# Late attention of a four-block fused kernel: the next rows' transpose moved from slot 7 to slot 0, queries and keys moved to the outputs' bank, the first rows one chunk sooner

## What is computed

```python
x = x + jnp.tanh(g_xattn[2]) * _L2_xattn_ref(_layernorm(x), ctx_512, ctx_512, Wc, bc)
x = x + jnp.tanh(g_ffn[2])   * _L2_ffn_ref(_layernorm(x), ...)            # top-2 of 8 low-rank experts
x = x + jnp.tanh(g_xattn[3]) * _L3_xattn_ref(_layernorm(x), ctx_512, Wq, Wkv_expand, Wout)
x = x + jnp.tanh(g_ffn[3])   * _L3_ffn_ref(_layernorm(x), ...)            # top-2 of 8 adapters

# L2: queries are the normalised rows, keys and values the context, 16 heads of 16
scores = jnp.einsum('bghsd,bgtd->bghst', qh, kh) * scale
# L3: qp = q @ Wq.T; k, v = split(latent_kv @ Wkv_expand.T); scores are causal
attn = jax.nn.softmax(jnp.where(causal, scores, min), axis=-1)
out = jnp.einsum('bhqk,bhkd->bhqd', attn, vh).reshape(b, sq, H) @ Wout.T
```

## Time and profile before

| | us |
|---|---|
| median of 3 runs | 814.8 (810.33 to 816.83) |
| the profiled execution, device time | 817.1 |
| its span, first to last instruction | 815.3 |
| PE busy in the span | 754.6 (93%) |
| late stage, first slot to the end of the span | 572.1 to 815.3 |
| mean granted PE clock | 0.971 of full speed |

### The profile page before, as it was taken

The page is one execution under the profiler, slowest core; times in us unless marked ns, Lnnn a source line. Parts: engine busy times, 40 slices in busy tenths (PEclk is TensorE's granted clock), DMA queues, the critical chain, the costliest instruction groups (busy, mean ns, idle before and its releaser), DMA issues.

```text
span 815.3 us, 13192 instructions
## 1 busy us (share of the span) xinstructions
PE 754.6 (93%) x4753; PEld 595.5 (73%) x4754; DVE 505.6 (62%) x1171; ACT 356.2 (44%) x1178; POOL 191.3 (23%) x230
## 2 busy tenths in 40 slices
PE   6899999999999999999997889998889898898986
PEld 3688888888888888767775656886556676676764
DVE  5757455976875735455558653432877675665853
ACT  2121112111111111567675565222988686677851
POOL 0000031000000000000005990234354644535110
PEclk9989999999999999999999899999999999999998
DMA  8856100000003000400000004002222175275200
GB/s 245 302 162 211 25 0 1 1 1 0 1 1 107 1 0 1 146 1 1 2 1 2 1 10 63 1 1 72 72 72 66 42 109 94 69 117 98 66 15 26
DMA packets 53409, 44.95 MB, mean 55 GB/s; under 512 B 6641, under 2 KB 48609, under 8 KB 53217
## 3 DMA queue, kind: packets, MB, share of 16 engines
q1 hardware_dynamic: 53344, 44.11, 20.9%
HBM read 37.94 MB, written 6.16 MB: 54 GB/s over the span
## 4 chain that ended last, share of the span: by engine, by line
PE 74%; ACT 11%; DVE 8%; issue 4%; POOL 1%; DMA 1%; SPq 1%; ACTq 0%; POOLq 0%; DVEq 0%
PE PS L1679 22%; PE PS L1705 11%; ACT arena L1001 4%; PE PS L1768 3%; PE PS L1844 3%; ACT arena L931 3%; PE PS L1933 3%; PE PS L1784 2%; PE PS L1800 2%; PE PS L1812 2%; PE PS L1859 2%; PE PS L1827 2%; ACT arena L811 2%; PE PS L1959 2%; PE PS L2022 2%
## 5 line engine op out<-in xcount | busy, mean ns | idle before, releaser
L625 POOL TENSOR_TENSOR RS<-MV,eps 128x2 f32<-128x2 f32 x32 | 6.3, 197 | 546.3 <-DVE MV L1114 448.6
L811 ACT ACTIVATE arena<-PS 128x256 f32<-128x256 f32 (+3 forms) x192 | 102.7, 565 | 66.8 <-PE PS L1768 37.6
L1001 ACT ACTIVATE arena<-PS,W_d 128x256 f32<-128x256 f32 (+1 forms) x256 | 111.4, 460 | 13.3 <-DVE W_d L1395 11.2
L871 ACT ACTIVATE tanh_g<-PS 128x512 f32<-128x512 f32 x48 | 28.7, 597 | 170.1 <-PE PS L1679 170.1
L1679 PE MATMUL PS<-XT,W_g 128*128 128x256 f32 (+1 forms) x400 | 97.6, 387 | 0.0
L1679 PE MATMUL PS<-XT,W_u 128*128 128x256 f32 (+1 forms) x400 | 95.0, 379 | 0.0
L1705 PE MATMUL PS<-W_d,mlp_tmp 128*128 128x256 f32 (+1 forms) x400 | 93.9, 380 | 0.0
L1679 PEld LDWEIGHTS PS<-XT,W_u 128*128 128x128 f32 (+1 forms) x400 | 75.6, 190 | 11.2
L1705 PEld LDWEIGHTS PS<-W_d,mlp_tmp 128*128 128x128 f32 (+1 forms) x400 | 75.6, 190 | 10.3
L1679 PEld LDWEIGHTS PS<-XT,W_g 128*128 128x128 f32 (+1 forms) x400 | 75.2, 192 | 10.6 <-issue 0.8
L931 ACT ACTIVATE arena<-PS,arena 128x256 f32<-128x256 f32 x128 | 58.9, 477 | 15.4 <-DVE arena L1341 13.3
(11 more groups left out here) (226 smaller groups left out, 1362.3 us busy)
## 6 DMA issues: line engine op xcount, KB each, us to landing
NW<-scratch SPq DMA_DIRECT2D x64, 64.0 KB, 2.4
PM<-scratch SPq DMA_DIRECT2D x64, 64.0 KB, 2.4
W_d<-in_w_d SPq DMA_DIRECT2D x1, 3072.0 KB, 10.6
scratch<-W_d SPq DMA_DIRECT2D x16, 192.0 KB, 3.8
arena<-in_wq SPq DMA_DIRECT2D x4, 512.0 KB, 7.3
arena<-in_wo1T SPq DMA_DIRECT2D x4, 512.0 KB, 9.2
W_g<-in_w_g SPq DMA_DIRECT2D x2, 1024.0 KB, 12.5
W_u<-in_w_u SPq DMA_DIRECT2D x2, 1024.0 KB, 14.5
```

The source lines that it names most:

```text
L811: last = act.activation(dst, src, ACT.Copy)
L1001: last = act.activation(PL[:, n % 2, k * S:k * S + w], PS[:, bank + x, i * S:i * S + w], ACT.Exp, bias=NML[:, n % 2, k:k + 1], accum_out=D ...
```

## The change

- The transpose of the next rows is no longer issued two rounds ahead in slot 7 (and once in slot 0 of round 0), but for every round r+1 in slot 0 of round r, behind that slot's transposes and values. ACT copies it out behind the exponentials of slot 0.
- The query projection of the next causal round moves from slot 0 to slot 1, behind its transposes, and from bank 7 to bank 6. ACT copies it out at the head of slot 2.
- The keys move from slot 6 to slot 5, to bank 6, and are copied out at the head of slot 6, no longer ahead of its exponentials.
- POOL splits every round's queries at the head of its round r loop; SP issues queries r+1, then keys r+2. Two waits are added for the keys: SP's for `key_stacked` of the keys before and for the last scores of round r-2, POOL's for `key_stored`.
- The rows of round 0 are transposed behind chunk 16 and not 17, and split into `KP` in place of `XB[0]`, which the ternary stage still reads.

```diff
@@ late_fills (the same moves stand in ACT's and PE's loops)
-        if n == 0:
-            order.append((7, "turn", 1, 0))
-        if p == 0 and ahead and causal(r + 1):
-            order.append((7, "q", r + 1, 0))
...
+        if p == 0 and ahead:
+            order.append((7, "turn", r + 1, 0))
+        if p == 1 and ahead and causal(r + 1):
+            order.append((6, "q", r + 1, 0))
...
-        if p == 6 and r + 2 < ROUNDS and causal(r + 2):
-            order.append((7, "k", r + 2, 0))
+        if p == 5 and r + 2 < ROUNDS and causal(r + 2):
+            order.append((6, "k", r + 2, 0))
...
-        if p == 7 and r + 2 < ROUNDS:
-            order.append((7, "turn", r + 2, 0))
...
-TERNARY_TURN = [b * CH1 + 2 for b in range(NB - 1)] + [(NB - 1) * CH1 - 1]
+TERNARY_TURN = [b * CH1 + 2 for b in range(NB - 1)] + [(NB - 1) * CH1 - 2]
@@ SP
             def stack_keys(r):
                 sp.wait_ge(key_parts, r - NB + 1)
+                if r > NB:
+                    sp.wait_ge(key_stacked, 16 * len(PRODUCTS) * (r - NB))
...
+                bank, value = fill_at("late", "s", r - 2, PAIRS - 1)
+                sp.wait_ge(filled[bank], value)
...
             stack_queries(0)
-            stack_queries(1)
             for r in range(ROUNDS - 1):
-                if causal(r + 1):
-                    stack_queries(r + 1)
-                if r + 2 < ROUNDS:
-                    if causal(r + 2):
-                        stack_keys(r + 2)
-                    else:
-                        stack_queries(r + 2)
+                stack_queries(r + 1)
+                if r + 2 < ROUNDS and causal(r + 2):
+                    stack_keys(r + 2)
@@ ACT
-                if n == 0:
-                    late_queries(1)
-                if p == 0 and ahead and causal(r + 1):
+                if p == 2 and ahead and causal(r + 1):
                     late_queries(r + 1)
+                if p == 6 and r + 2 < ROUNDS and causal(r + 2):
+                    evacuate("late", "k", r + 2, 0,
+                             (KC[r % 2], PS[:, 6, :].rearrange("p (c s) -> p c s", c=2)))
...
                 if n + 2 < ITEMS:
                     late_exponents(n + 2)
+                if p == 0 and ahead:
+                    if causal(r + 1):
+                        xt_out(fill_at("late", "turn", r + 1)[1], (r + 1) % 2)
+                    else:
+                        late_queries(r + 1)
@@ PE
+                if p == 0 and ahead:
+                    late_turn(r + 1)
+                if p == 1 and ahead and causal(r + 1):
+                    late_query(r + 1)
...
-                if p == 6 and r + 2 < ROUNDS and causal(r + 2):
+                if p == 5 and r + 2 < ROUNDS and causal(r + 2):
                     late_keys(r + 2)
                 if p == 7:
                     denominators_turn(r)
-                if p == 7 and r + 2 < ROUNDS:
-                    late_turn(r + 2)
```

More of the change, by code:

```diff
@@ L577, in stack_queries @@
                     sp.dma_start(q_store[r % 2][:, c * P:(c + 1) * P, :].rearrange("k p t -> p k t"),
-                                 XB[r % 2][:, :, c * S:(c + 1) * S]).then_inc(query_stored[c], 16)
+                                 (XB[r % 2] if r else KP)[:, :, c * S:(c + 1) * S]).then_inc(query_stored[c], 16)
                 for c in range(2):
@@ L730, in query_parts_of @@
                 for c in range(2):
-                    x, (high, mid, low) = XT[r % 2][:, c, :], [XB[r % 2][:, k, c * S:(c + 1) * S] for k in range(3)]
+                    x, (high, mid, low) = XT[r % 2][:, c, :], [(XB[r % 2] if r else KP)[:, k, c * S:(c + 1) * S] for k in range(3)]
                     at = 3 * (2 * r + c)
@@ L745, in key_parts_of @@
                 pool.wait_ge(drained[bank], value)
+                if r > NB:
+                    pool.wait_ge(key_stored, 16 * (r - NB))
                 at = 3 * (r - NB)
@@ L762, in _ @@
             add_bias(1, bc_2)
-            query_parts_of(1)
             for r in range(ROUNDS + 1):
-                if r + 1 < ROUNDS and causal(r + 1):
+                if r + 1 < ROUNDS:
                     query_parts_of(r + 1)
@@ L779, in _ @@
                         add_bias(r + 2, bc_2)
-                        query_parts_of(r + 2)
         @block.scalar
@@ L1061, in _ @@
                     evacuate("late", "o", (n - 1) // PAIRS, c, (OTR[:, c, :], PS[:, 6, 0:S]))
-                if p == 6 and r + 2 < ROUNDS and causal(r + 2):
-                    evacuate("late", "k", r + 2, 0,
-                             (KC[r % 2], PS[:, 7, :].rearrange("p (c s) -> p c s", c=2)))
                 if p == 7:
                     evacuate("late", "den_turn", r, 0, (RDT, PS[0:NH, 7, 0:S]))
-                if p == 7 and r + 2 < ROUNDS:
-                    if causal(r + 2):
-                        xt_out(fill_at("late", "turn", r + 2)[1], r % 2)
-                    else:
-                        late_queries(r + 2)
                 if n + 2 < ITEMS:
                     late_exponents(n + 2)
+                if p == 0 and ahead:
[3 more added lines that the diff above has]
+                        late_queries(r + 1)
                 if p == 4 and ahead and causal(r + 1):
@@ L2097, in _ @@
                     late_scores(n + 2)
-                if n == 0:
-                    late_turn(1)
-                if p == 0 and ahead and causal(r + 1):
-                    late_query(r + 1)
                 if p == 1 and r:
```

## The result

The changed kernel takes 827.9 us (median of 4 runs, 825.8 to 830.4) beside 815.8 of the kernel before (810.3 to 817.9, 4 runs): ratio 1.016, 95% interval 1.010 to 1.022. It is slower by more than 1%, where I had forecast 818 with 824 as the upper end. The profiled execution took 827.6 us with a span of 825.8, 10.5 more than the span before; its mean granted clock is 0.968, before 0.971. PE is busy 756.1 us in place of 754.6, so nearly all of the difference is time in which PE stands still (both traces have stretches of slow clock, which largely cancel in this sum). A trace tells of one execution: of 19 runs of the kernel before, the fastest took 810.5 us at a mean granted clock of 0.985, the slowest 818.2 at 0.971.

A forecast was written before the change was run, and what follows sets the result against it. PE was taken to set the pace, through standstills and slow clock. Terms -1.2 (causal) + 2.1 (rounds 1 and 2) + 3.3 (round 1's queries) - 1.2 (first rows) + 0.5 (round 6) = +3.5 us on 814.8: 818, range 807 to 824.

The forecast's parts named there:

- The bank 6 moves cost nothing either: Queries and keys in bank 6: each earlier content is copied out before the next user comes, so no cost.
- the stall in slot 1: PE waits ahead of the denominators for ACT's copy of the rows: 1.9 us, six times, in rounds 1 to 6.
- Rounds 1 and 2: Denominators begin 1.05 us later in each: 2.1 us lost, up to 1 more each if the clock falls.
- I take it that the clock falls again: Causal rounds: slow clock, 1.5 us each, returns behind slot 1's stalls, leaving a gain of 0.3 each, 1.2 in all.
- the first rival: The clock does not fall behind the new stalls in slot 1: about 811 us, chance 0.22.
- The first rows: Round 0's rows, turned one chunk sooner in the ternary stage, shorten the later wait for stacks: 1.2 us gained.
- The keys' added waits: The two waits added on SP and POOL are fulfilled when reached: no cost.
- The queries of round 1: Slot (0,6): stacks come later, PE's wait grows from 1.33 to 3.6 us; with slow clock 3.3 us lost.
- round 6, where I had allowed 0.5: Round 6, with no keys in slot 5 and shorter slots: 0.5 us of wait for stacked queries, from 0 to 1.5.
- the chain: From POOL's start on the queries to the stacks that PE waits for: 12.3 us.
- could give at most: Upper limit in the steady part: slot 7's turns cost 9.8 us of waits plus 6 of slow clock, about 16.
- The third rival: Stacked queries come too late in rounds 3 to 5, 3.1 us of wait each: 827 us, chance 0.13.

The follow-up runs named there:

- e2: The changed kernel, but ACT copies the projected queries in slot 1, ahead of the expert weights' copy and that slot's exponentials: 819.9 us, ratio 1.006.
- d1: The changed kernel, but DVE does the choice of experts in slot 0 behind that slot's maxima, not in slot 7 ahead of them: 821.8 us, ratio 1.006.
- w1: The changed kernel, but POOL waits for the maxima of the next slot 0 before it splits the keys: 828.4 us, ratio 1.019.
- f10: The changed kernel with ten unused matmuls into bank 6 where PE waits in slot 1 for the rows' copy, six times: 819.0 us, ratio 1.004.
- e4: The kernel before, with only the rows of round 0 turned one chunk sooner and split into KP: 814.1 us, ratio 0.997.
- e3: The changed kernel, but round 1's rows are turned and copied at the head of slot 0 of round 0, as before: 824.8 us, ratio 1.010.
- k6: The kernel before, with only the keys moved to slot 5 and bank 6, the turn left in slot 7: 806.4 us, ratio 0.988.
- e123: The changed kernel with turned rows copied ahead of slot 0's exponentials, queries copied in slot 1, round 1's rows turned as before: 798.6 us, ratio 0.979.
- e1: The changed kernel, but in slot 0 ACT copies the turned rows ahead of that slot's exponentials: 802.8 us, ratio 0.983.
- e12: The changed kernel with turned rows copied ahead of slot 0's exponentials and projected queries copied in slot 1: 799.2 us, ratio 0.980.

## Why the prediction was wrong

Against the span, 10.5 us came where 3.5 were forecast. The direction and the main exchange (a stall in slot 7 for one in slot 1) were right, two steps were not, and the rest is size.

**The step that failed** is "The bank 6 moves cost nothing either: the outputs of slot 0 are copied before the queries come, the queries before slot 4". The next user of bank 6 behind the queries is not slot 4's output. The values of slot 2 fill it already, and between the projection and its copy ACT had the job's product and a set of exponentials. That makes four waits, 6.0 us, which the prediction had put at nothing. All four are gone in e2, which moves that one copy and is 8 us faster. I had looked at who ends in the bank, not at who begins in it.

**The term mis-sized** is the stall in slot 1. The stall itself is there six times in the place forecast, and 1.88 and 1.87 us of rounds 1 and 5 are what slot (7,0) gave. The other four are 2.23, 2.88, 2.47 and 2.77. That is 14.1 in place of 11.4. The profile that I read had no turn and no key splitting in slot (7,0), so I took ACT's list to be the only bound. In rounds 2, 3, 4 and 6 ACT waited 0.2 to 1.0 us for DVE's maxima, behind the job's choice; in three of these DVE itself was held by POOL's splitting of the keys. d1 takes all of it away, w1 the part due to POOL.

**Rounds 1 and 2.** Price 1.05 us each, and "with one up to 1 more each", one being a fall of the clock. Round 1 came out at it (4.48 with the queries, forecast 4.35). The stretch from (1,3) to (2,3) cost 3.85: 1.05, 0.3 for the longer stall, 1.0 for the clock at 0.53 behind it, as allowed, and 1.6 for the fall in slot (1,6), behind a wait that the change did not make. That last part is chance as far as the traces show.

**The clock.** "I take it that the clock falls again": it fell at four of the six stalls in slot 1 (rounds 2, 3, 5 and 6), and stayed at 1.00 behind those of 1.88 us in round 1 and 2.47 in round 4. So (3,3) to (4,3) is the one causal round that became shorter, by 1.0 us. f10 prices the falls at 9 us. The choice was right for three of the four causal rounds that I took it for, and the first rival (no fall, 811) is refuted.

**What was right.** The first rows: -1.25 for -1.2, and no slow clock behind their stacks (e4; the agreement to 0.05 us is luck, as such traces differ by 2 us at this slot). The keys' added waits cost nothing that a trace shows. The queries of round 1: PE's wait for PM 3.33 us for 3.6 (e3). No wait at L1627 for a copy in slot 7, one of 1.78 us for DVE's rows at the last ternary turn. No wait for stacks in rounds 3 to 5, and none in round 6, where I had allowed 0.5. But not by the sum that I gave: ACT copied the queries late, so POOL started 12.5 to 17.0 us into the rounds and not at 11.7. The scores came 11.0 to 13.8 us behind POOL's start and found the stacks there, in round 6 in less than the 12.3 us of the chain that I had reckoned with. The stalls and the slow clock had held back the scores as well as the queries, so two errors covered each other, which is luck. And what the change "could give at most", 16 us: k6 alone gets 10 of them, e123 some 17. The gain was real, and came back on PE as 14.1 + 6.0 us of new waits with slow clock behind.

**The third rival** gave 827 us and the result is 827.9, yet its mechanism, late stacks in rounds 3 to 5, did not happen. A fitting total proves no mechanism. Its chain does come up, but in e1, e123 and w1, when other waits have moved.

The sum over the failed steps, with their measured size: 3.5 + 6.0 (values) + 2.7 (denominators) + 1.0 (clock behind round 2's stall) + 1.6 (clock in slot (1,6)) - 0.5 (round 6) - 1.75 (tail) = 12.5, against 10.5. Of the 2.0 too many, 1.7 are the projection of round 4 without a fall, 1.89 us in place of 3.59 before; the rest stays open.

## What to carry over

When an operation moves to another buffer of PE's output, list every user of that buffer in order and ask of each whether its first write comes ahead of the copy that empties it, with that copy's place in the evacuating engine's own list. Here two copies by ACT that lay one set of exponentials (some 1.6 us) too late cost 29 us (827.9 to 799.2, e12), waits and the slow clock with them, and the same change with both moved forward is 17 us faster than the kernel before. Where a change has parts that do not need each other, price and try each alone: the keys' move gave 10 us without the turn's. And do not lean on a fall of the clock that one trace shows: the same 1.3 us of waiting left it alone in one trace and had it fall in another.

## What the runs showed of the hardware

- The length of a standstill does not decide alone whether PE's clock falls. In one execution it fell to 0.55 behind 1.87 us (721.0 to 724.0), and stayed at 1.00 behind 1.88 us (599.0 to 601.0) and behind 2.47 us (691.6 to 695.0). It was 0.50 from 616.0 to 618.0, behind a wait of 1.29 us, and 1.00 behind the same wait of 1.30 us in the kernel before. What else decides stays open. The Trainium skill (TensorE: Matmul & The Clock Gate, section "Why this matters for your kernels") warns of idle gaps over some 3 us. As a bound the traces disagree with it, since gaps of 1.3 to 2.9 us were followed by a fall.
- Ten matmuls without use in each of six waits of 1.9 to 2.9 us kept the clock at 1.00 behind all of them, and were worth 9 us here (f10).
- From the issue of the queries' first store on SP's queue to their first read back it took 2.8 us with nothing just in front (changed kernel, four times; SP issues the second store in this time), and 4.8 to 6.8 us with the keys' eight read-backs just ahead (w1 and e123).
- A DVE operation with two inputs in SBUF that starts within a two-input operation of POOL ends with it: 0.93 us for 16 columns, otherwise 0.17 to 0.20, seen three times in the changed kernel, four times in the one before, and gone from this operation when POOL was moved (w1). The Trainium skill (SBUF — State Buffer, section "SBUF: two separate sides") says that the two engines share a port pair which the one that starts first holds for its whole instruction; the trace agrees. MATCH_REPLACE8, whose row has one input form, was not held: 0.15 us at 749.95, within the same POOL operation.
